# Four attention layers in one pipeline: other places for the products in a stage, another order of the setup

## What is computed

```
def layer0(x, kv):                       # rms-normalised inputs
    xn, kvn = rmsnorm(x, gq), rmsnorm(kv, gkv)
    a = softmax(q(xn) k(kvn)^T / sqrt(8)) v(kvn)
    return xn + a @ wo.T + bo
def layer1(x, kv, mask):                 # biases, mask, layer norm
    a = softmax(where(mask, -inf, q k^T / sqrt(8))) v
    return layernorm(x + a @ Wo.T + bo)
def layer2(x, kv):                       # causal, feed forward with gelu
    h = layernorm(softmax(causal(q k^T / sqrt(8))) v + x)
    return gelu(h @ W1.T + b1) @ W2.T + b2 + h
def layer3(x, kv):
    return layernorm(softmax(q k^T / sqrt(8)) v + x)
```

## Time and profile before

| what | value |
|---|---|
| three timed runs | 1085.7 us median (1081.01 to 1086.39) |
| the profiled execution | 1088.03 us, of which the span of the trace is 1086.2 |
| busy: PE, DVE, ACT, POOL | 945.0, 856.5, 733.3, 369.8 us |
| mean granted clock of PE | 0.969 of 2.4 GHz |
| the last chain, by engine | PE 57%, DVE 24%, ACT 7%, issue 6%, POOL 4% |
| DMA | 73.74 MB, mean 68 GB/s |
| exponential on ACT (L1015) | 1152 of 511 ns in the mean |
| maximum on DVE (L1159) | 1056 of 565 ns in the mean |

### The profile page before, as it was taken

One profiled execution on the slowest core, in us unless ns is written; L12 is line 12 of the kernel. 1 busy time (PEld: TensorE's weight loads), 2 busy tenths in 40 slices (PEclk: granted clock), 3 DMA queues, 4 the chain that ended last, 5 costly groups with the idle time before them and its releaser, 6 DMA issues.

```text
span 1086.2 us, 43882 instructions
## 1 busy us (share of the span) xinstructions
PE 945.0 (87%) x18826; PEld 555.8 (51%) x18826; DVE 856.5 (79%) x1800; ACT 733.3 (68%) x1644; POOL 369.8 (34%) x387
## 2 busy tenths in 40 slices
PE   0679989999989999999989898988888898989996
PEld 0235555555555555555555454555545454555653
DVE  4787887887877898889886877878787978779852
ACT  1146767767767787778766676767667676777776
POOL 5854344434323113311351515252524243321100
PEclk9787999999999999999998999999999999999999
DMA  8232213213212323332231212121212122021200
GB/s 211 76 83 85 61 53 85 77 51 84 71 50 84 101 64 90 91 101 55 81 96 31 88 42 71 32 71 32 77 35 77 37 68 77 27 84 50 55 5 6
DMA packets 63641, 73.74 MB, mean 68 GB/s; under 512 B 8131, under 2 KB 59115, under 8 KB 63319
## 3 DMA queue, kind: packets, MB, share of 16 engines
q1 hardware_dynamic: 63446, 70.92, 23.2%
HBM read 50.35 MB, written 18.15 MB: 63 GB/s over the span
## 4 chain that ended last, share of the span: by engine, by line
PE 57%; DVE 24%; ACT 7%; issue 6%; POOL 4%; SPq 1%; DMA 1%; POOLq 0%; ACTq 0%; DVEq 0%
PE ring L592 21%; PE acc L760 13%; PE sexp L592 12%; DVE mx L1159 9%; PE ring L635 5%; DVE mneg L1165 4%; DVE mx L1157 3%; ACT probs L1015 2%; POOL kbd L510 2%; PE ring L817 1%; PE ring L612 1%; DVE kp L1136 1%; SPq L471 1%; PE ring L771 1%; DVE ssq L1121 1%
## 5 line engine op out<-in xcount | busy, mean ns | idle before, releaser
L1159 DVE TENSOR_TENSOR mx<-ring,mx 120x400 f16<-120x400 f32 (+1 forms) x1056 | 560.2, 565 | 142.9 <-PE ring L592 138.6
L1015 ACT ACTIVATE probs<-sexp 120x400 f32<-120x400 f32 (+1 forms) x1152 | 533.7, 511 | 169.0 <-PE sexp L592 164.7
L592 PE MATMUL ring<-qx,krep 96*32 96x400 f16 (+2 forms) x4608 | 411.0, 346 | 38.8 <-DVE mx L1159 15.6
L592 PE MATMUL sexp<-qx,krep 97*32 97x400 f16 (+2 forms) x4608 | 407.4, 340 | 10.1 <-ACT probs L1015 6.2
L760 PE MATMUL acc<-probs,vx 120*18 120x200 f32 (+1 forms) x4608 | 254.3, 337 | 0.9 <-ACT probs L1015 0.7
L592 PEld LDWEIGHTS ring<-qx,krep 96*32 96x32 f16 (+2 forms) x4608 | 131.0, 98 | 127.6 <-DVE mx L1159 38.2
L592 PEld LDWEIGHTS sexp<-qx,krep 97*32 97x32 f16 (+2 forms) x4608 | 130.7, 96 | 103.8 <-ACT probs L1015 37.8
L527 POOL TENSOR_TENSOR qx<-qs,headmask 96x400 f16<-96x400 f16 x96 | 79.7, 860 | 262.6 <-DVE qs L1146 262.6
L760 PEld LDWEIGHTS acc<-probs,vx 120*18 120x18 f32 (+1 forms) x4608 | 131.0, 99 | 69.2 <-issue 5.0
L494 POOL TENSOR_TENSOR ct<-ctf,ct 128x480 f16<-128x480 f32 (+1 forms) x72 | 80.9, 1123 | 5.8
L635 PE MATMUL ring<-wv,ct 128*120 128x128 f16 (+1 forms) x864 | 64.1, 224 | 14.4 <-ACT vx L978 11.6
(11 more groups left out here) (133 smaller groups left out, 889.2 us busy)
## 6 DMA issues: line engine op xcount, KB each, us to landing
krep<-kept SPq DMA_DIRECT2D x144, 120.0 KB, 2.6
ctf<-in_ctxT SPq DMA_DIRECT2D x16, 722.0 KB
kept<-kp SPq DMA_DIRECT2D x48, 240.0 KB, 2.9
krep<-kept SPq DMA_DIRECT2D x72, 121.0 KB, 2.9
kept<-kp SPq DMA_DIRECT2D x24, 242.0 KB, 2.8
nat<-in_ctx SPq DMA_DIRECT2D x8, 720.0 KB
maskexp<-maskmax SPq DMA_DIRECT2D x8, 281.2 KB, 3.5
anymask<-in_mask SPq DMA_DIRECT2D x1, 1128.1 KB, 7.0
```

Of the source, the lines that this page charges most:

```text
L592: last = run(out[g:g + m], w[:, g:g + m], x, **flags)
L1015: act.activation(probs[0:r, j % PR, :], sexp[j % SR][0:r, 0:QW], ACT.Exp).then_inc(sem["probs_ready"], 1)
L1159: op = dve.tensor_tensor(dst, src, dst, ALU.max)
```

## The change

1. The tables place the products at other steps. Before and after: k0 9, 10; k1 12, 22; k2 15, 30; OT 13, 12; wo 16, 15; xT 17, 18; q 19, 20; v0 22, 24; v1 24, 27; v2 26, 33; mk0 28, 25; mk1 30, 28; mk2 32, 31; scale 30, 32. The sums of squares on DVE had been bound to v2 (steps 29 and 32); they get a name of their own, `power`, at 25 and 28. Layer 2 likewise, see the diff.
2. The bytes of the mask are turned into bf16 by POOL, once per stage, instead of by ACT four steps ahead of each mask tile.
3. SP issues the transposed context first, then keys 0, its replication, keys 1 and 2, the second replication, then the store.
4. The constants get semaphores by need (`ident_in`, `wk_in`, `x_in`, `const_in`) and another order. For the first unit alone ACT writes the high part of the context straight from PSUM and DVE the low part, in place of ACT's copy and POOL's two instructions; DVE squares its first four chunks. ACT runs one small exponential at the start.
5. DVE prepares the weights of the keys and x first, the values' weights after the third group of keys of stage -2, and the rest in steps 0 to 6 of stage 1; POOL clears the tiles of the values after stage -2.

```diff
-AT = {"ct0": 0, "ct1": 3, "ct2": 6, "O": 7, "k0": 9, "k1": 12, "OT": 13, "k2": 15, "wo": 16, "xT": 17, "q": 19,
-      "v0": 22, "v1": 24, "v2": 26, "mk0": 28, "mk1": 30, "mk2": 32, "scale": 30, "mt0": 36, "mt1": 37, "mn": 41}
+AT = {"ct0": 0, "ct1": 3, "ct2": 6, "O": 7, "k0": 10, "OT": 12, "wo": 15, "xT": 18, "q": 20, "k1": 22, "v0": 24,
+      "mk0": 25, "v1": 27, "mk1": 28, "k2": 30, "mk2": 31, "v2": 33, "power": 25, "scale": 32, "mt0": 36, "mt1": 37, "mn": 41}
-AT2 = {"cx": 4, "kqv": 7, "s0": 17, "s1": 19, "s2": 21, "s3": 23, "e0": 27, "e1": 28, "e2": 29, "e3": 30,
-       "pt0": 31, "pt1": 33, "pt2": 34, "pt3": 35, "a": 42, "o": 44, "out": 45}
-AT2_FF = {"out": 0, "scale": 13, "at": 18, "h": 23, "w2": 29}
+AT2 = {"cx": 2, "kqv": 5, "s0": 23, "s1": 25, "s2": 26, "s3": 28, "e0": 29, "e1": 31, "e2": 32, "e3": 34,
+       "pt0": 32, "pt1": 34, "pt2": 35, "pt3": 38, "a": 42, "o": 44, "out": 45}
+AT2_FF = {"out": 0, "scale": 12, "at": 16, "h": 19, "w2": 27}
...
# SP, stage
                 if s.prep is not None:
-                    for g in range(3):
-                        keep_keys(s.prep, g)
-                    replicate(s.prep, 0, s.exp, NSTEP // 3)
...
+                    keep_keys(s.prep, 0)
+                    replicate(s.prep, 0, s.exp, NSTEP // 3)
+                    keep_keys(s.prep, 1)
+                    keep_keys(s.prep, 2)
+                    replicate(s.prep, 1, s.exp, 2 * NSTEP // 3)
...
# SP, constants
+                for name, dst, src in (("ident_in", ident[:, :], ident_in[0]), ("ident_in", cols[:, :], cols_in),
+                                       ("wk_in", wk[:, :, :], w_qkv[:, :, T * PARTS:T * PARTS + D].rearrange("l c n -> c l n")),
+                                       ("x_in", xall[:, :, :], x_in.rearrange("b s d -> s b d")),
+                                       ("x_in", wq[:, :, :, :], w_qkv[:, :, 0:T * PARTS].rearrange("l c (t p) -> c l t p", t=T)),
+                                       ("x_in", headmask[:, :], headmask_in), ("x_in", rows[:, :, :], rows_in),
+                                       ("const_in", wv[:, :, :], w_qkv[:, :, T * PARTS + D:T * PARTS + 2 * D].rearrange("l c n -> c l n")),
...
# POOL
+            def mask_bytes(u):
+
+                pool.wait_ge(*at("mask_loaded", u, 16))
+                for g in range(3):
+                    _, c0, n, _ = groups()[g]
+                    pool.tensor_copy(maskb[:, c0:c0 + n], mask8[:, c0:c0 + n]).then_inc(sem["mask_copied"], 1)
...
+            pool.wait_ge(sem["x_power"], 1)
+            pool.tensor_tensor(rinvx[:, :], ssqx[:, :], half[0:S, 0:B], ALU.pow).then_inc(sem["x_root"], 1)
+            pipeline(UNITS, stage, first=-2, last=-2)
             for i in range(2):
                 pool.memset(vx[:, i, :, :], 0.0).then_inc(sem["pool_ready"], 1)
...
# PE
-            pe.wait_ge(sem["const_in"], 16 * 15)
+            pe.wait_ge(sem["ident_in"], 32)
...
# ACT, context(u, g, before)
+                if u is UNITS[0]:
+                    act.mul(ct[:, 0, 0, c0:c0 + n], bank(f"ct{g}", u)[:, 0:n], cols[:, COLC["gkv"]:COLC["gkv"] + 1]
+                            ).then_inc(sem["ct_high"], 1)
+                    return
...
# DVE
+            def context(u, g):
+
+                _, c0, n, _ = groups()[g]
+                dve.wait_ge(*at("ct_high", u, g + 1))
+                dve.scalar_tensor_tensor(out=ct[:, 0, 1, c0:c0 + n], in0=bank(f"ct{g}", u)[:, 0:n],
+                                         scalar=cols[:, COLC["gkv"]:COLC["gkv"] + 1], in1=ct[:, 0, 0, c0:c0 + n],
+                                         op0=ALU.mult, op1=ALU.subtract).then_inc(sem["ct_low"], 1)
...
# DVE, stage
+                    if s.prep is UNITS[0]:
+                        for g in range(3):
+                            if j == AT[f"ct{g}"]:
+                                context(s.prep, g)
+                        if j == AT["k0"] - 2:
+                            input_scaled()
+                        if j == AT["k2"] + 2:
+                            values_weights()
+                    if s.exp is UNITS[1]:
+                        rest(j)
...
             pipeline(UNITS, stage, last=-3)
+            keys_weights()
+            input_power()
             pipeline(UNITS, stage, first=-2)
```

More of the change, by code:

```diff
@@ L551, in stage @@
             def stage(s, n):
-                if s.prep is not None:
+                if s.prep is not None and s.prep is not UNITS[0]:
                     for g in range(3):
@@ L560, in stage @@
                     root(s.post)
+                if s.prep is not None and s.prep.L == 1:
+                    mask_bytes(s.prep)
                 if s.load is not None and s.load.L == 0:
@@ L581, in _ @@
             pool.memset(v2[:, :, DH:DH + 1], 1.0).then_inc(sem["pool_ready"], 1)
-            pool.wait_ge(sem["x_power"], 1)
-            pool.tensor_tensor(rinvx[:, :], ssqx[:, :], half[0:S, 0:B], ALU.pow).then_inc(sem["x_root"], 1)
-            pipeline(UNITS, stage, first=-2)
+            pipeline(UNITS, stage, first=-1)
         def grouped(run, out, w, x, **flags):
@@ L1082, in stage @@
                         queries(s.prep)
-                    for g in range(3):
-                        if s.prep is not None and s.prep.L == 1 and j == AT[f"mk{g}"] - 4:
-                            mask_bytes(s.prep, g)
                     layer2(s, j)
@@ L1103, in _, with step @@
             counted = {}
+            steps = [0]
+            def step(op):
+                steps[0] += 1
+                op.then_inc(sem["setup"], 1)
+                dve.wait_ge(sem["setup"], steps[0])
+            def context(u, g):
[4 more added lines that the diff above has]
+                                         op0=ALU.mult, op1=ALU.subtract).then_inc(sem["ct_low"], 1)
@@ new lines, in values_weights, with rest @@
+            def values_weights():
+                dve.wait_ge(sem["const_in"], 16 * 8)
+                split(wv[:, :, :], wv16[:, 0], wv16[:, 1]).then_inc(sem["wv_ready"], 1)
+                dve.memset(ones[:, :], 1.0)
+            def rest(j):
+                if j == 0:
+                    step(dve.tensor_scalar(bq[:, :, :], bq[:, :, :], SCALE, None, ALU.mult))
+                    step(dve.tensor_copy(bq16[:, :, :], bq[:, :, :]))
+                if j == 1:
+                    dve.scalar_tensor_tensor(out=bq16[:, :, :], in0=bq16[:, :, :], scalar=which[:, QW:QW + 1], in1=bq[:, :, :],
+                                             op0=ALU.mult, op1=ALU.add)
+                if j == 2:
+                    dve.tensor_copy(which16[:, :], which[:, 0:QW])
+                if j == 3:
+                    dve.tensor_copy(heads16[:, :], heads[:, :])
+                    dve.tensor_copy(identb[:, :], ident[:, :])
+                if j in (4, 5):
+                    dve.tensor_scalar(masked_by[:, j - 4, :], ident[:, :], MASKED[j - 4], None, ALU.mult)
+                if j == 6:
+                    dve.tensor_scalar(bq2[:, :], cols[:, COLC["bq2"]:COLC["bq2"] + 1], SCALE, None, ALU.mult
+                                      ).then_inc(sem["rest_ready"], 1)
@@ L1335, in stage @@
                     for part in range(2):
-                        if s.load is not None and s.load.L == 0 and j == AT["v2"] + 3 + 3 * part:
+                        if s.load is not None and s.load.L == 0 and j == AT["power"] + 3 * part:
                             power(s.load, part)
@@ L1341, in stage @@
                     layer2(s, j)
-            steps = [0]
-            def step(op):
-                steps[0] += 1
-                op.then_inc(sem["setup"], 1)
-                dve.wait_ge(sem["setup"], steps[0])
             dve.memset(krep[PARTS:PARTS + 1, :, :, :].rearrange("o a t k -> o (a t k)").bitcast(F32), TWO_ONES
```

104 lines of the change are left out of this document (49 added, 55 removed).

## The result

Before: 1085.6 us median (1081.0 to 1086.4, four runs). After: **1052.9 us** (1052.0 to 1053.6, four runs), ratio 0.971, 95% interval 0.968 to 0.974. That is inside the range of 1020 to 1070 and 7.9 us above the forecast of 1045. The profiled execution took 1052.0 (span 1050.2), 36.0 less than the profiled one of before (1088.0).

The account below looks back on a forecast made before the run. TensorE was taken as the fullest engine after the fill, its idle time the ceiling. Terms 8.4-1.4+8.4+7.3+2.4+15.8+1.0=41.9 gave 1046.1 from the profiled 1088.0 and 1043.8 from the median 1085.7; forecast 1045, range 1020 to 1070.

Parts of the forecast that it names:

- The fill: Start up to the first exponential: PE no longer waits for 15 constants, first maximum at about 36.0; 8.4 us gained.
- (a): Projection to step 15, x's transpose to 18: PE's waits for DVE's addition go; 8.4 us in stages 1 to 11.
- (b): Sums of squares four steps earlier, so DVE catches up before the transposes of the maxima; 7.3 us in stages 0 to 4.
- (d): Stages 12 to 19: waits for values, addition and part of the maxima go, less 4.0 for DVE's queries; 15.8 us gained.
- The moved setup: Small DVE instructions moved into steps 0 to 6 of stage 1; charged 1.4 us, bounds 0 to 3.8.
- (c): Mask casts leave ACT for POOL: 2.4 us gained in stages 6 to 11, bounds 0 to 6.8.
- rival D: ACT's block at step 19 stops DVE, PE idles and its clock falls; 6.0 us a stage lost, 1110 us; chance 0.04.
- the signs that the prediction set itself: Stages 12 to 19 at 48 to 49.5 us; wrong if 50, under 47, or clock at 0.50 more than once or twice.
- the 5.6 credited for the maxima: Stages 12 to 19: half of 11.2 us of DVE low parts for k1 and k2, moved out of steps 8 to 17.
- B: Rival: in stages 12 to 19 the lumps only change places; nothing from (c), (d) or stage 20; 1065 us, chance 0.17.
- C: Rival: PE's idle time in stages 12 to 19 falls to 2.0 a stage, 38.8 gained instead of 15.8; 1023, chance 0.17.
- The 4.8 us: Possible cost of (c) by the skill: eight stages with casts, each holding one DVE addition for 0.6 us; not forecast.

Follow-up runs that it names:

- experiment 3: Changed kernel with the 24 mask casts back on ACT instead of POOL, four steps ahead of each mask product: 1051.8 us, ratio 0.969.
- experiment 8: Changed kernel with layer two's feed-forward activation block at step 24 instead of 19 and its second product at 29 instead of 27: 1034.2 us, ratio 0.954.
- experiment 2: Changed kernel with only layer two's step tables (AT2, AT2_FF) as before the change: 1055.4 us, ratio 0.973.
- experiment 12: On experiment 8: output product at step 4, layer two's cx at 5, kqv at 8, feed-forward scale at 18, its product at 20: 1027.0 us, ratio 0.947.
- experiment 4: Changed kernel with ACT's feed-forward activation block one step later, at 20 instead of 19: 1059.2 us, ratio 0.978.
- experiment 5: Changed kernel with each of POOL's two 2.88 us multiplications for layer two's keys cut into four: 1054.7 us, ratio 0.972.
- experiment 6: Changed kernel with POOL's square root for layer two's norm moved ahead of the two key multiplications: 1063.6 us, ratio 0.981.
- experiment 7: Changed kernel with POOL's root moved ahead of layer two's key multiplications and these cut into four each: 1069.0 us, ratio 0.987.
- the probe: Changed kernel with one extra POOL instruction ahead of layer two's multiplications: none for batches 0 and 1, a power for 2, memsets for 3 to 7: 1054.4 us.

## Why the prediction came out as it did

**Right.** The fill: 8.0 gained of 8.4, with the first maximum at 34.25 where I had 36.0 and the transposes at 17.3 (17.0). The steps on the way were each off by up to 2.2 us and partly cancel: x landed at 17.24, not 15.0 (DVE stood 4.82 for the rows), its root came at 20.0+1.64=21.6 (22.0), x was ready at 25.3 (26.0, though the terms listed there, 1.95+0.95+1.21+1.49 from 19.7, give 25.3), the spreading at 33.3 (33.0). Stages 0 to 5: 9.8 of 9.8. The waits that (a), (b) and (d) named went: 12.1 to 0.5 for the addition of the projected output, no wait of PE on the transposes of the maxima left in stages 0 to 4, the 9.6 for the values gone. The moved setup lengthened stage 1 by 1.6 (38.3 against 36.7 in stages 2 to 4) where I had 1.4. That the sums were right stage by stage rests on one execution of each, in which a window of low clock moves 1.7 us. In the twelve experiments, whose start is the same, the fill took 74.6 to 76.2 us and stage 1 began at 112.6 to 115.9 (113.8 in the changed kernel, 124.8 before).

**Wrong in size, both ways.** Term (c), 2.4, measured 0 (experiment 3; its interval would hide some 5 us, but stages 7 to 11 are equal to 0.1 us each). The bound of 0 was the right end: the casts, 0.59 us each on either engine, seem to fall into ACT's idle time once the tables leave some. Stages 6 to 11 gained 11.6 instead of 7.0 all the same, 6.2 of it without the tables: 1.9 in stage 6 go with a low clock in the one execution of before, and which part of the remainder made the other 4.2 is open. Stage 12 gained 10.8 where an eighth of (d) is 2: about 5 was the clock's fall, which I had listed in the earlier trace rows as the price in rival D and not seen as a sum to be won back.

**What the sum hides.** The time lies in the range, and the sum of 41.9 is only 5.9 over the 36.0 of the profiled executions, in part by luck: stages 13 to 19 fell 17.7 short, while stages 6 to 12 gained 13.4 more than forecast, some 7 of it because the clock fell in stages 6 and 12 of the profiled execution of before and not after. (Its mean clock was 0.969; other executions of the same kernel show up to 0.983, so that fall need not be in each.) By the signs that the prediction set itself, its middle was wrong: stages 12 to 19 took 50.2 us each, not 48 to 49.5, and the granted clock was at 0.50 in ten windows within them.

**The step that failed** is in (d): "Against it: DVE's instruction on the queries at step 20 now stands behind ACT's block ... 0.5 us more of idle DVE per stage, 4.0", and, tied to it, the 5.6 credited for the maxima. Measured in stages 13 to 19: DVE's wait rose by 13.6 (20.2 less 6.6), 1.9 a stage, and the waits for the maxima didn't fall but rose by 2.9. I had the mechanism, in this term and as rival D, down to the falling clock, and priced it at a quarter here and too high there (6.0 a stage; moving the block from 19 to 24 in experiment 8 is worth 17/7=2.4). From the rows of before it could have been sized better: the block is 1.28+1.05+1.28=3.6 us, an exponential ahead of it 0.5, and four banks at 0.5 us a maximum (2.02 for four in the earlier trace rows) cover 2.0: an estimate of 2.1 us a stage, clock aside.

**The second fault** was to judge the block's old place by its cost alone. At step 23 it cost 9.6 in seven stages as v1 stood right behind; I took the 9.6 as the gain of moving it, and not what the old place had held up: cover. Experiment 8 moves it back to 24 with the values spread around it and has both. Its place isn't all: experiment 2 has the block at 23 with the new values' places and layer two's other steps old, and won nothing in these stages.

**The rivals.** B (1065: nothing in the middle) describes stages 13 to 19 well (51.4 us each after 50.8), but not stages 6 to 12. C (1023, the idle time spreads to 2 a stage) is not this kernel; experiment 12 comes near its time, with 26.0 us idle in seven stages, 3.7 each, at a clock of 0.99.

The Trainium skill's "SBUF — State Buffer", section "Who interferes with whom", which I had weighed against (c), says that a DVE instruction with two SBUF inputs and a GpSimd instruction that reads SBUF exclude each other for one instruction. The 4.8 us that I worked out from it for the casts aren't seen: DVE is busy 184.8 us in stages 6 to 11 with the casts on GpSimd and 184.5 with them on ACT. Three additions there did meet a cast, against my "come after the casts", and took 0.30, 0.40 and 0.64 us instead of 0.28. What it says of one instruction agrees with the trace at the multiplications (0.83 and 2.46 us beside 2.88) and falls short after a power (4.15 to 5.20 us), for which the measurement decides.

## What to carry to other kernels

A block that can't be cut on one engine belongs, as experiments 4 and 8 suggest, where the bound engine has work that needs nothing from it, and behind the small instruction for which a third engine waits; price each place by both. When idle time on TensorE falls and its busy time rises for the same matmuls, look at the granted clock: in stage 15, stops of 1.6 and 2.8 us were followed by two windows at 1.2 GHz that cost 3.4 us more. And when one wait is cut, ask what stands behind it in the same queue: experiments 2, 4, 5, 6 and 7 each cut a named wait and won nothing.

## What the runs showed of the hardware

A DVE addition with two SBUF inputs that meets GpSimd's multiplications of 2.88 us gets in at the end of the running one: it takes 0.82 us, 2.15 in the kernel before, though the second is queued, and 2.46 when it meets the second. With GpSimd's power directly ahead of them it gets in only when all are through: 4.33 us with two (seven stages of experiment 6), 5.20 with eight short ones (experiment 7), 4.15 in the probe's one batch. In stage 12 of experiments 6 and 7, where no power stands ahead, the same instruction got in early. Why a power does this, the rows don't say; a memset there doesn't (1.06 to 1.46 us). That one instruction of another engine, 2 us earlier, sets whether a 0.28 us addition takes 0.8 or 5 us, I had not expected.

ACT's table load took 1.28 us each way with the activations directly behind (830.37+1.28=831.65, start 831.66).
